# Last attention of a 12-stage model: turned-back values in PSUM banks of their own, ScalarE's work in another order, stacks turned by identity products

## The reference

```python
mu = jnp.mean(x, axis=-1, keepdims=True)
var = jnp.mean(jnp.square(x - mu), axis=-1, keepdims=True)
xn = (x - mu) * jax.lax.rsqrt(var + EPS) * ln_g + ln_b
q = (xn @ Wq + bq).reshape(B, T, H, D // H)
k = (xn @ Wk + bk).reshape(B, T, H, D // H)
v = (xn @ Wv + bv).reshape(B, T, H, D // H)
scale = 1.0 / math.sqrt(D // H)
attn = jnp.einsum('bnhd,bmhd->bnmh', q, k) * scale
w = jax.nn.softmax(attn, axis=2)
y = jnp.einsum('bnmh,bmhd->bnhd', w, v).reshape(B, T, D)
```

## Time and profile before

| what | value |
|---|---|
| median of 3 runs | 2624.93 us |
| the profiled execution's own time | 2637.31 us |
| its span, first to last instruction | 2635.2 us |
| mean granted TensorE clock, whole span | 0.843 |
| last attention, by its first and last instructions | about 2260 to 2538.5 us, 278.5 us |
| granted clock in it | 0.63 |
| turn of the first half of q_shifted moved by ACT, unit after unit | at 2290.52, 2317.57, 2349.53, 2382.09, 2415.09, 2448.37, 2480.95, 2514.04 us |

### The profile page before, as it was taken

How to read it: one execution, slowest core, us unless ns; L and a number is a source line. 1 busy time by engine, 2 the same in 40 slices (tenths; PEclk the granted TensorE clock), 3 DMA queues, 4 the chain that set the end, 5 groups by cost and what they waited for, 6 DMA issues and landing times. The chain is left out here.

```text
span 2635.2 us, 40558 instructions
## 1 busy us (share of the span) xinstructions
PE 2160.3 (82%) x13860; PEld 1691.5 (64%) x13860; DVE 1468.8 (56%) x3930; ACT 1000.2 (38%) x2247; POOL 131.4 (5%) x191
## 2 busy tenths in 40 slices
PE   3588777766997788499899989999979997588875
PEld 2344444435996322399899967888879995355543
DVE  6633334365666899756632226777742227655547
ACT  2244333333222332122244435555534444333434
POOL 2100000020000100100000000000000000000000
PEclk9776756677998899599989989999979998666678
DMA  5000000000000000000000004444300000000000
GB/s 155 2 1 0 0 1 0 0 28 1 1 0 1 0 0 0 32 1 0 1 1 0 0 19 132 125 125 124 123 12 0 0 0 0 1 1 0 0 1 16
DMA packets 47119, 59.65 MB, mean 23 GB/s; under 512 B 7089, under 2 KB 44689, under 8 KB 46323
## 3 DMA queue, kind: packets, MB, share of 16 engines
q1 hardware_dynamic: 47023, 58.43, 7.3%
HBM read 32.20 MB, written 26.21 MB: 22 GB/s over the span
## 5 line engine op out<-in xcount | busy, mean ns | idle before, releaser
L701 ACT ACTIVATE m2a_hid<-psum,m_b 128x256 f32<-128x256 f32 x256 | 100.2, 474 | 114.6 <-PE psum L55 114.5
L701 ACT ACTIVATE m2b_hid<-psum,m_b 128x256 f32<-128x256 f32 x256 | 100.2, 474 | 114.6 <-PE psum L55 114.5
L686 PE MATMUL psum<-m_w,m2a_hid 128*128 128x128 f32 x1024 | 126.2, 277 | 0.0
L686 PE MATMUL psum<-m_w,m2b_hid 128*128 128x128 f32 x1024 | 126.2, 277 | 0.0
L686 PEld LDWEIGHTS psum<-m_w,m2b_hid 128*128 128x128 f32 x1024 | 122.1, 194 | 0.6
L686 PEld LDWEIGHTS psum<-m_w,m2a_hid 128*128 128x128 f32 x1024 | 122.1, 194 | 0.6
L719 DVE SCALAR_TENSOR_TENSOR m2b_acc<-psum,m2b_gates,m2b_acc 128x128 f32<-128x128 f32 x128 | 39.0, 347 | 148.7 <-PE psum L686 148.7
L719 DVE SCALAR_TENSOR_TENSOR m2a_acc<-psum,m2a_gates,m2a_acc 128x128 f32<-128x128 f32 x128 | 39.0, 347 | 148.3 <-PE psum L686 148.3
L2026 ACT ACTIVATE a_p<-a_p,a_nmax 128x256 f32<-128x256 f32 x128 | 64.0, 500 | 143.3 <-DVE a_nmax L2053 143.3
L1769 DVE TENSOR_REDUCE a_nmax<-psum 128x2 f32<-128x512 f32 x128 | 83.0, 687 | 50.3 <-PE psum L1610 50.3
L1056 DVE TENSOR_TENSOR_SCAN a1s_clamped<-a1s_clamp_coef,a1s_bounds 128x1024 f32<-128x1024 f32 x48 | 108.6, 2265 | 0.0
(11 more groups left out here) (608 smaller groups left out, 5728.7 us busy)
## 6 DMA issues: line engine op xcount, KB each, us to landing
a_scratch<-a_pos SPq DMA_DIRECT2D x64, 384.0 KB, 2.7
a_shifted<-a_scratch SPq DMA_DIRECT2D x64, 256.0 KB, 3.1
m_w<-in_m_w SPq DMA_DIRECT2D x1, 2048.0 KB
arena<-in_m_w SPq DMA_DIRECT2D x1, 2048.0 KB, 9.2
arena<-in_m_up SPq DMA_DIRECT2D x1, 1760.0 KB, 7.1
a_w<-in_a_w SPq DMA_DIRECT2D x1, 1536.0 KB, 7.8
out<-X SPq DMA_DIRECT2D x1, 1024.0 KB, 5.1
m_down<-in_m_down SPq DMA_DIRECT2D x1, 880.0 KB
```

The costliest lines, as they stand in the source:

```text
L686: last = nc.tensor.matmul(ps_y(e % 2)[:, t * D:(t + 1) * D], hid[:, e % 2, c * SEQ + t * P:c * SEQ + (t + 1) * P], m.m2_w2[:, e, c, :], st ...
L701: last = nc.scalar.activation(hid[:, e % 2, c * SEQ:(c + 1) * SEQ], ps_up(e % 2)[:, c * SEQ:(c + 1) * SEQ], ACT.Gelu, bias=m.m2_b1[:, e * ...
```

## The change

The turned-back values no longer share bank 6 with the values: turn_back(0) and (1) write bank 7, turn_back(2) and (3) bank 5. values(j) now waits only until ACT has moved values(j-1). The banks 5 and 7 have other users, so turn_back, turn_shifted (first half) and the second quarter of turn_stack get waits for these. The steps are placed anew in the groups: turn_back(0) in group 4, turn_back(1) in group 6, turn_back(2) in group 0 and turn_back(3) in group 2 of the next unit; values(0) stands ahead of start_b. ACT takes the exponential first in each group, and moves values one group later than before. DVE normalises (0) and (1) behind the maxima of groups 4 and 6, (2) and (3) in groups 1 and 2 of the next unit, and end_b follows start_d. The 24 turns of st per unit become products of an F32R tile with an F32R identity (ident_r), where they were float32 transposes.

```diff
-        ps_av, ps_back = m.psum[:, 6, 0:SEQ], m.psum[:, 6, SEQ:2 * SEQ]
+        ps_av = m.psum[:, 6, 0:SEQ]
+        ps_back = lambda j: m.psum[:, 7 if j < 2 else 5, 0:SEQ]
...
-                        last = nc.tensor.transpose(out[:, j, t * P:(t + 1) * P], st[:, t, a, heads, :].rearrange("p h f -> p (h f)").bitcast(F32),
-                                                   m.ident[:, :])
+                        last = nc.tensor.matmul(out[:, j, t * P:(t + 1) * P], st[:, t, a, heads, :].rearrange("p h f -> p (h f)"), ident_r[:, :],
+                                                start=True, stop=True)
...
                 for r in range(4):
+                    if r == 1 and (not isinstance(n, int) or n > 1):
+                        pe.wait_ge(o_ready, 4 * n - 4)
...
                 pe.wait_ge(shift_ready, 2 * n + half + 1)
+                if half == 0 and (not isinstance(n, int) or n):
+                    pe.wait_ge(o_ready, 4 * n - 2)
...
                 if j or not isinstance(n, int) or n:
-                    pe.wait_ge(o_ready, 4 * n + j)
+                    pe.wait_ge(av_moved, 4 * n + j)
...
                 pe.wait_ge(av_moved, 4 * n + j + 1)
+                if j in (1, 3):
+                    pe.wait_ge(o_ready, 4 * n + j)
+                elif j == 0 and (not isinstance(n, int) or n < NB - 1):
+                    pe.wait_ge(moved, 4 * n + 7)
+                elif j == 2 and (not isinstance(n, int) or n < NB - 1):
+                    pe.wait_ge(nmax_ready, HEADS * n + 2 * HEADS)
...
                     if g == 0 and prev:
+                        turn_back(1 - u, n - 1, 2)
                         values(1 - u, n - 1, 3)
-                    if g == 1 and prev:
+                    if g == 2 and prev:
                         turn_back(1 - u, n - 1, 3)
+                    if g in (4, 6):
+                        turn_back(u, n, g // 2 - 2)
+                    if g in (2, 4, 6):
+                        values(u, n, g // 2 - 1)
                     if g == 1 and next:
                         start_a(1 - u, n + 1)
                     if g == 2 and next:
                         start_b(1 - u, n + 1)
-                    if g in (2, 4, 6):
-                        values(u, n, g // 2 - 1)
...
-                    if g in (3, 5, 7):
-                        turn_back(u, n, g // 2 - 1)
...
                 for g in range(GROUPS):
+                    exps(n, g)
                     if g == 1:
                         move_shifted(u, n, 1)
-                    exps(n, g)
-                    if g == 0 and prev:
+                    if g == 1 and prev:
                         move_values(1 - u, n - 1, 3)
-                    if g in (2, 4, 6):
+                    if g in (3, 5, 7):
                         move_values(u, n, g // 2 - 1)
...
                     if g == 1 and prev:
+                        normalise(1 - u, n - 1, 2)
+                    if g == 2 and prev:
                         normalise(1 - u, n - 1, 3)
                         end_a(1 - u, n - 1)
-                    if g == 2 and prev:
-                        end_b(1 - u, n - 1)
                     if g == 3 and next:
                         start_c(1 - u, n + 1)
-                    if g == 3:
-                        normalise(u, n, 0)
-                    if g == 3 and next:
                         start_d(1 - u, n + 1)
+                    if g == 3 and prev:
+                        end_b(1 - u, n - 1)
...
-                    if g in (5, 7):
-                        normalise(u, n, g // 2 - 1)
+                    if g in (4, 6):
+                        normalise(u, n, g // 2 - 2)
```

More of the change, by code:

```diff
@@ L1542, in full_attention @@
         kT, q_plain, q_shifted = sbr("kT", [P, 2, 4, SEQ]), sbr("q_plain", [P, 4, SEQ]), sbr("q_shifted", [P, 4, SEQ])
+        ident_r = sbr("ident_r", [P, P])
         va = sb("va", [P, 2, PAIR, HEADS, STRIP])
@@ L1641, in turn_back @@
                 pe.wait_ge(av_moved, 4 * n + j + 1)
+                if j in (1, 3):
[4 more added lines that the diff above has]
+                    pe.wait_ge(nmax_ready, HEADS * n + 2 * HEADS)
                 for t in range(PAIR):
-                    last = nc.tensor.transpose(ps_back[:, t * P:(t + 1) * P], ov[:, j % 2, t * P:(t + 1) * P], m.ident[:, :])
+                    last = nc.tensor.transpose(ps_back(j)[:, t * P:(t + 1) * P], ov[:, j % 2, t * P:(t + 1) * P], m.ident[:, :])
                 last.then_inc(back_ready, 1)
@@ L1684, in tail @@
             def tail(u, n):
+                turn_back(u, n, 2)
                 values(u, n, 3)
@@ L1780, in normalise @@
                 dve.wait_ge(back_ready, 4 * n + j + 1)
-                back = ps_back.rearrange("p (t k f) -> p t k f", t=PAIR, f=STRIP)
+                back = ps_back(j).rearrange("p (t k f) -> p t k f", t=PAIR, f=STRIP)
                 nc.vector.reciprocal(rec[:, :, :], back[:, :, :, HD])
@@ L1795, in first @@
                 dve.wait_ge(m.loaded["a3"], m.total["a3"])
+                nc.vector.tensor_copy(ident_r[:, :], m.ident[:, :])
                 nc.vector.memset(va[:, :, :, :, :], 1.0)
@@ L1835, in unit @@
                         shift(1 - u, n + 1, 0)
-                    if g in (5, 7):
-                        normalise(u, n, g // 2 - 1)
+                    if g in (4, 6):
+                        normalise(u, n, g // 2 - 2)
             def tail(u, n):
+                nc.vector.drain()
+                normalise(u, n, 2)
                 normalise(u, n, 3)
```

## The result

The kernel is slower: 2666.44 us (median of four runs, 2659.02 to 2669.99) against 2624.98; the medians lie 41.5 us apart. The measured ratio, which I use throughout, is 1.0131, with a 95% interval of 1.0107 to 1.0155, or about +34 us; the stage in the traces, 33.1 us longer, agrees with it. That is the side I forecast, but past the end of my range (2652).

A forecast was written before the change was run, and what follows sets the result against it. No engine was full; PE's one queue with short waits, and its clock, set a unit's length. The sum at unchanged clock, +3.5 us, plus +6.7 for the clock gave +10, carried to the median 2635, range 2614 to 2652.

The forecast's parts named there:

- (a): Maxima 15 to the stack: turn_back(2) +0.07, cheaper turns -0.40, start_c uncovered by the new order +1.35 us.
- (b): From the stack to the first plain product: +0.15 us per unit at an unchanged clock.
- (c): Plain products 0 to 7: turn_back(1) leaves PE, normalise(0) enters on DVE; -0.1 us (0 to -0.4).
- (d): To maxima 8: the wait of values(2) goes, turn_back(1) comes in; -0.94 us.
- (e): Maxima 8 to 12: turn_shifted now waits for normalise(1), delaying plain 12; +0.45 us (+0.25 to +0.85).
- As single-pass products I take 0.65: Four turns of turn_shifted, 1.05 us as transposes, would take 0.65 as products, within 0.45 to 1.0.
- 1.9 ... in half of 7 units: +6.7: Clock term: the lost or late rise costs 1.9 us per unit, in half of 7 units, +6.7 us.
- the stack is paced by ACT, so it loses little: Within the clock term: the stack's turns, paced by ACT, would lose little at the lower clock.
- the gap: PE idle ahead of the stack, about 2 us, would delay or lose the clock's rise in many units.
- Rival 2: Clock lost in every unit and products cost what transposes do: +24 us, 2649; chance 0.14.
- Rival 1: Clock unaffected, as the stack could bring the rise back each time: 2628.5 (2621 to 2632); chance 0.20.
- Rival 3: Faster: the clock rises before start_b in more than half of the units: -10 us, 2615; chance 0.22.

The follow-up runs named there:

- e5: The kernel before with one edit: values(0) stands ahead of start_b on PE, turns still transposes; ratio 1.0050 to the kernel before.
- e6: The changed kernel with normalise(1) moved between the maxima of heads 9 and 10; ratio 1.0093 to the kernel before.
- e2: The changed kernel with the 24 turns per unit as float32 transposes again; ratio 1.0051 to the kernel before.
- e3: The kernel before with only the 24 turns per unit made single-pass products; ratio 1.0059 to the kernel before.
- e13: The changed kernel with the stack alone turned by transposes again, shifted rows still by products; ratio 1.0093 to the kernel before.
- e11: The kernel before with single-pass products in the stack alone, shifted rows still turned by transposes; ratio 1.0073 to the kernel before.
- e1: The changed kernel with start_b ahead of values(0) on PE again; ratio 1.0058 to the kernel before.
- e8: The changed kernel with start_b ahead of values(0), transposes again, and normalise(1) after the maximum of head 9; ratio 0.9952 to the kernel before.
- e4: The changed kernel with two unused f32 products on PE ahead of the wait for start_c; ratio 1.0052 to the kernel before.

## Why the prediction was wrong

One unit, from the end of maxima 15 to the same point a unit later, in the steps of the prediction (us, mean of units 1 to 7, read from the two traces; the forecast is at an unchanged clock; the stretches not listed, maxima 8 to 11 and behind plain 12, did not change):

| step | before | changed | difference | forecast |
|---|---|---|---|---|
| (a) to the first turn of the stack | 10.94 | 12.60 | +1.66 | +1.02 |
| (b) to the first plain product | 4.22 | 7.32 | **+3.10** | +0.15 |
| (c) to the end of maxima 7 | 6.35 | 6.54 | +0.19 | -0.10 |
| (d) to maxima 8 | 3.81 | 2.94 | -0.87 | -0.94 |
| (e) end of maxima 11 to plain 12 | 0.67 | 1.52 | +0.85 | +0.45 |
| whole unit | 32.56 | 37.48 | +4.92 | +0.58 |

*Waits (steps a, d, e): right.* The stack waits 2.17 us (about 2 forecast), the values' waits are gone, the turns wait 1.19 for normalise (1.3). e5 puts 7.1 us of idle time on the order, and e6 takes 9.5 off with the normalise wait.

*The price of a turn (step a, "As single-pass products I take 0.65"): wrong.* It is 1.04, which makes up most of what (a) and (e) exceed the forecast by. I read it from rows 9, a product of another shape; here nothing was saved. The upper end of my bound (1.0) was the answer. The Trainium skill, "TensorE: Matmul & The Clock Gate", LDWEIGHTS, whose rule made the saving zero, agrees with the trace in that. The sizes differ: by its 107 ns for a load, and a product as long, four would take an estimated 0.86 us, and they took 1.04.

*The clock: the step that failed.* I took "1.9 ... in half of 7 units: +6.7". It was lost in all seven units (v takes 1.16 in each), and the price is step (b): 3.10 us longer, nearly two thirds of what a unit grew by. One term of that price I had at nearly nothing, for a wrong reason. I held that "the stack is paced by ACT, so it loses little"; PE ran the stack without a pause, and it took 3.28 us in the mean where it had taken 2.32. In sum the busy time grew by 28.1, 4.0 per unit; that lies in the bounds I gave for a unit (0.87 to 5.7), but the choice was too low twice, and it put the forecast outside its range. That the forecast named the slower side rests on the waits, which came, and on a clock lost in half of the units.

The reason for the loss was also half wrong. I blamed the gap alone. e2 has the gap, and nearly the busy time of before; e3 has no new gap, and 21.3 us more. For the gap to cost the whole stretch it takes the products, as none of their 28 stacks at 0.50 was followed by the rise in time. With transposes the rise comes behind the stack, and e2 pays mostly in idle time.

*Rival 2 had the mechanism in part,* clock lost in every unit and turns as dear as transposes, and 2649 was short because it too took 1.9 a unit. *Rival 1* argued that sixteen cold turns bring the rise back: true of transposes (e2, e13), not of products (e11). I weighed only that the turns would be shorter. *Rival 3* needed the rise ahead of start_b; in the changed kernel values(0) took 1.94 in all seven units. With transposes in the same order (e2) the early rise did come in three of seven.

I set against rival 3 that transposes do raise the clock, against the Trainium skill, "TensorE: Matmul & The Clock Gate", Part 4, by which they do not count as busy. e2, e3 and e11 agree with rows 7 and go further: here the transposes are followed by the rise, and the products are the kind that is not. I never asked this of the new operation.

By parts, as differences of ratios: e6 puts 0.38% on the normalise wait, e1 0.73% on the order, e2 0.80% on the products; with all three taken away a gain of 0.5% is left (e8). It belongs to the banks, to the order that goes with them and to ScalarE's new order together, as no run takes these apart. The parts add up to 0.994, and e8's 0.9952 agrees with that within the noise.

## What to carry to other kernels

Before an operation on a throttled engine is swapped for an equivalent one, compare not only its duration but the clock in the stretch behind it, in one run of the swap alone: in the unit shown, e3's rows were equal to 0.01 us up to the stack, and the kernel still took 0.6% longer. Split the length of a stage into busy and idle time first: where busy grows at an equal instruction count, look for the clock, not for a wait. A change of several parts can hide a good one: the separate banks, with the order that goes with them, were worth 0.5% here, under 1.8% of other costs.

## What the hardware did that I had not expected

- A single-pass identity product of 128 by 128 takes as long as an f32 transpose at both clocks: four in 1.04 and 1.05 us at 0.50, sixteen in 2.01 and 2.00 at 1.00.
- 3.4 us of transposes at 0.50 were followed by 1.00 (before, e2, e13); as many products of the same length were not (changed kernel, e11). What in the product makes the difference is open: the two differ in data type and in kind of operation, and no run here separates these. One thing the traces show: the weight load of a turn takes 330 ns as a product (e3, a stack at 0.50) and 228 as a transpose (e2), at 1.00 191 and 141 (e3, before). Whether that is the cause is not shown.
- Work that nobody needs made the kernel faster (e4 against the changed kernel, 0.79%), as it ran in a wait and the products behind it were then at 1.00. Six of e4's units took 34.1 to 34.2 us, the changed kernel's 37.2 to 38.0.
